# A 16-batch cross-attention and expert feed-forward kernel: the first five steps in another order with products of zeros, and the output projection in front of the scores from step 6

## The chip, the core and the metric

One core of a Trainium2 chip runs the kernel. Its engines each work through a queue of their own: TensorE (PE; PEld is its weight load), VectorE (DVE), ScalarE (ACT), GpSimd (POOL) and SyncE (SP), which here only issues transfers (DMAs). The metric is the time of one execution on the device in microseconds (us), as the median of several runs.

## The reference

For each of 16 batches, with 256 tokens and 128 features:

```python
x = x + xattn(layernorm(x), ctx, ctx, Wq, bq, Wk, bk, Wv, bv, Wo, bo)   # 16 heads of 8 features, 64 keys
h = layernorm(x)
e = argmax(h.mean(axis=1) @ Wr + br)                                    # one expert of 8 for the whole batch
x = x + relu(h @ W1[e] + c1[e]) @ W2[e] + c2[e]                         # 512 hidden features
```

Everything is float32.

## The kernel before, in words

The work is a pipeline by hand. Each engine has a program of its own, written as a loop over steps t = -3 to 21, and in each step it does its share of several batches at different stages; semaphores tie the engines together. In step t, TensorE does for batch t the score product whose maximum is wanted (`scores_for_max`, L627, into banks a to d of PSUM), for batch t-2 the product of probabilities and V (`heads_product`, L645, into bank_g), for batch t-1 the scores that go to the exponential (`scores_t`, L682, banks e, f, a, b), for batch t-3 the output projection (`project_o`, L695, bank_g), for batch t+1 the projection of q (`project_q`, L708), the transposes of maxima and layernorms (L723, L749, L784), and for batch t-5 the two products of the expert (`up` L735, `down` L763). RAMP = 5 separates the first steps, in which the projection of q stands earlier, from the others.

The maximum takes a way of its own: VectorE reduces the scores (`reduce_max`, L877), TensorE transposes the result, ScalarE copies it (`max_transposed`, L514), and SyncE sends it into `q_stack`, whose rows are the operand of `scores_t`. There q stands split in a high and a low part (`high_q` L483 on ScalarE, `low_q` L937 on VectorE), also sent by SyncE. `q_stack` has two buffers. K is split in the same way in four pieces of four batches (`project_k`, `high_k`, `low_k`, `stack_k`), placed per head in `k_all` (`place_k`) and masked into `k_diag` (`diag_k`, on GpSimd and, for the last piece, ScalarE). V is projected in four pieces (`project_v` L603) and copied by ScalarE (`v_of` L460) into a frame that GpSimd fills first (`fill_v` L381).

ScalarE in a step t of 5 and more: the copy of the heads out of bank_g (`copy_heads` L498, batch t-2), the exponentials of batch t-1 in four groups (L490), `high_q`, `max_transposed`, four relus of batch t-5 (L530), a first layernorm (`normalise_x` L474), and copies of transposes. SyncE then takes the heads apart into `denom` and `numer` (`split_heads`); VectorE inverts (`invert_sums` L946), GpSimd multiplies (`normalise_heads` L398). VectorE adds the output projection to x plus bias (`add_x1` L903) and takes statistics; GpSimd makes the second layernorm of them (`norm2`, L359 to L368), and that is transposed (L784), summed for the choice of the expert (`logits`, `route_best`), and multiplied by the weights of the expert, which SyncE has loaded (`load_expert`).

What sets the order around the change is the order of the calls in each engine's loop, and the waits in front of each call. `project_o` has these, and they are not changed:

```python
pe.wait_ge(attn_done, n + 1)
if live(n + 1):
    pe.wait_ge(heads_out, n + 2)
```

`heads_out` counts the copies of the heads by ScalarE: the projection of batch t-3 waits for the copy of batch t-2 in the same step, as the projection writes bank_g, which that copy reads. `transpose_max` waits for the first two exponentials of batch t-1, since it shares bank_f with the scores.

Of the kernel before, what the change touches and what calls it, by code (L numbers as in the profile page):

```python
# [6 lines left out]
F32 = mybir.dt.float32  # L7
F32R = mybir.dt.float32r
# [23 lines left out]
def xattn_moe_kernel(nc, x, ctx_t, consts, experts, out):  # L32
# [13 lines left out]
    with ExitStack() as ctx:  # L46
# [8 lines left out]

        cst = sb("cst", [P, CONST_W])
# [4 lines left out]
        eps_sb = sb("eps_sb", [P, QT])  # L61
        table_in = sb("table_in", [P, QT])
# [13 lines left out]
        q_stack = sb("q_stack", [P, 2, SLOTS, TOK], F32R)  # L76
# [9 lines left out]
        numer = sb("numer", [P, TOK])  # L86
        denom = sb("denom", [P, TOK])
# [39 lines left out]
        def flat(bank):  # L127
# [5 lines left out]
        STATS_AT = {-3: (0, 1), -1: (2,), 0: (3, 4), 1: (5, 6), **{t: (t + 5,) for t in range(2, B - 5)}}  # L133
        SCALE_AT = {-3: ((0, 1), (1, 2)), -1: ((2, 3),), 0: ((3, 4),), 1: ((4, 6),),
                    **{t: ((t + 4, t + 5),) for t in range(2, B - 4)}}
        XN_AT = {0: (2,), 1: (3,), 2: (4,), 3: (5, 6), **{t: (t + 3,) for t in range(4, B - 3)}}
        RAMP = 5

        def late(n):
            return n + 4 < RAMP  # L140

# [5 lines left out]
        kstack_in = [sem(f"kstack_in{k}") for k in range(B // PIECE)]  # L147
        qstack_in = [sem(f"qstack_in{k}") for k in range(2)]
        max_in = [sem(f"max_in{k}") for k in range(2)]
# [6 lines left out]
        qzero_done = sem("qzero_done")  # L156
        klo_done = sem("klo_done")
# [20 lines left out]
        kdiag_act = sem("kdiag_act")  # L178
# [23 lines left out]

        half_set = sem("half_set")
# [15 lines left out]

        def live(n):  # L220
            return 0 <= n < B

# [6 lines left out]
        def _(sp):  # L229
# [9 lines left out]
            def stack_k(c):  # L239
                cols = cols_of(c)  # L240
                if c == 0:
                    sp.wait_ge(kzero_dve, 1)
                else:
                    sp.wait_ge(kzero_pool, 1)
                sp.wait_ge(khi_done, c + 1)
                for row in range(2):
                    sp.dma_start(k_stack[row::4, :, cols], k_parts[:, 0, cols].bitcast(F32)
                                 ).then_inc(kstack_in[c], 16)
                sp.wait_ge(klo_done, c + 1)
                sp.dma_start(k_stack[2::4, :, cols], k_parts[:, 1, cols].bitcast(F32)).then_inc(kstack_in[c], 16)  # L250

            def stack_q_high(n):
                par = n % 2
# [3 lines left out]
                if n >= 2:  # L257
                    sp.wait_ge(s_done, GROUPS * (n - 1))
                for row in (0, 2):
                    sp.dma_start(q_stack[row::4, par].bitcast(F32), q_parts[:, par, 0, :].bitcast(F32)  # L260
# [787 lines left out]
```

## Time and profile before

| what | value |
|---|---|
| median of 3 runs | 180.39 us (179.39 to 180.77) |
| the profiled execution's own time | 179.66 us |
| its span, first to last instruction | 177.8 us |
| TensorE busy | 147.7 us, 83% of the span |
| VectorE, ScalarE, GpSimd busy | 121.5, 113.9, 105.2 us |
| mean granted TensorE clock | 0.914 of full |

The span is from the first instruction to the last; the execution's own time has 1.9 us more around it. Busy time is an average over three stages: the first steps, the steady steps and the end. A granted clock of 1.00 is 2.4 GHz, of 0.50 is 1.2 GHz. In a row of the timeline the square brackets say how long the engine had been idle before, and what ended that.

### The profile page before, as it was taken

To read this page: it belongs to the slowest core of one execution; us is meant where nothing else is said; L and a number is where in the kernel's file an instruction comes from. 1 tells how busy PE (TensorE), PEld (TensorE's weight loads), DVE (VectorE), ACT (ScalarE), POOL (GpSimd) and SP (SyncE) were. 2 spreads that over 40 slices of the span, in tenths; PEclk is the share of its full clock that TensorE was granted. 3 is DMA by queue.
4 is the path that set the end of the run, shared out by engine and by line. 5 is a ranking of instruction groups with operands and counts; after the bars stand their busy time and mean duration, and the time that the engine had idled before them with its cause. 6 is when DMAs were issued, how large, how long until landed. Compare 5 with 4: busy or idle time off the path is not lost.

```text
span 177.8 us, 4066 instructions
## 1 busy us (share of the span) xinstructions
PE 147.7 (83%) x1194; PEld 108.8 (61%) x1194; DVE 121.5 (68%) x334; ACT 113.9 (64%) x281; POOL 105.2 (59%) x186
## 2 busy tenths in 40 slices
PE   0495678748873999999999999999999989878893
PEld 0273344416342687777778787787877667566583
DVE  6694846283926889898979989797786937263200
ACT  3325565858876597896969778696766748234340
POOL 6567279311908485959586685956648293676300
PEclk9998755795765699999999999999999999999999
DMA  5838324492024254647455553646556452454150
GB/s 171 204 137 250 119 94 151 96 316 70 30 94 139 90 182 163 195 128 238 142 192 187 175 196 133 217 123 236 166 183 197 149 166 81 161 176 128 66 168 30
DMA packets 25014, 27.27 MB, mean 153 GB/s; under 512 B 4512, under 2 KB 20768, under 8 KB 24992
## 3 DMA queue, kind: packets, MB, share of 16 engines
q1 hardware_dynamic: 23136, 26.13, 45.3%
q10 hardware_dynamic: 1856, 0.88, 1.9%
q8 instruction: 10, 0.16, 0.4%
q14 instruction: 12, 0.10, 0.2%
HBM read 12.58 MB, written 2.10 MB: 83 GB/s over the span
## 4 chain that ended last, share of the span: by engine, by line
PE 65%; ACT 11%; DVE 5%; POOL 5%; issue 5%; DMA 5%; SPq 2%; ACTq 0%; POOLq 0%; DVEq 0%
PE bank_g L763 15%; PE bank_g L645 9%; PE bank_c L735 6%; PE bank_q L708 5%; PE bank_g L695 5%; PE bank_a L627 4%; PE bank_e L682 4%; PE bank_d L735 4%; ACT probs_t L490 3%; POOL xn L368 3%; DMA x_sb<-in_x 3%; PE bank_a L682 2%; ACT hid_t L530 2%; DMA ew<-in_experts 2%; PE bank_e L749 2%
## 5 line engine op out<-in xcount | busy, mean ns | idle before, releaser
L763 PE MATMUL bank_g<-ew,hid_t 128*128 128x128 f32 x256 | 32.4, 280 | 2.1 <-ACT hid_t L530 2.0
L763 PEld LDWEIGHTS bank_g<-ew,hid_t 128*128 128x128 f32 x256 | 29.8, 192 | 6.6 <-issue 6.0
L946 DVE RECIPROCAL inv_sum<-denom 128x256 f32<-128x256 f32 x16 | 27.7, 1731 | 0.2
L368 POOL TENSOR_SCALAR xn<-x,mv,rstd 128x128 f32<-128x128 f32 x32 | 25.2, 795 | 1.7
L359 POOL TENSOR_TENSOR ve<-mv,eps_sb 128x2 f32<-128x2 f32 x16 | 3.1, 195 | 38.3 <-DVE mv L916 38.3
L645 PE MATMUL bank_g<-probs_t,v_all 128*32 128x256 f32 x256 | 19.6, 430 | 1.6 <-DVE k_parts L840 1.2
L867 DVE TENSOR_TENSOR y_sb<-bank_g,x_b 128x256 f32<-128x256 f32 x16 | 6.8, 425 | 20.1 <-PE bank_g L763 20.1
L498 ACT COPY heads_sb<-bank_g 128x512 f32<-128x512 f32 x16 | 9.4, 586 | 16.5 <-PE bank_g L645 16.4
L530 ACT ACTIVATE hid_t<-bank_c,ew 128x256 f32<-128x256 f32 x32 | 13.4, 472 | 8.6 <-PE bank_c L735 8.3
L405 POOL TENSOR_TENSOR x_b<-x,ew 128x256 f32<-128x256 f32 x16 | 11.6, 727 | 10.9 <-DMA ew<-in_experts 10.4
L735 PE MATMUL bank_c<-xn_t,ew 128*128 128x256 f32 x64 | 16.7, 383 | 0.0
L735 PE MATMUL bank_d<-xn_t,ew 128*128 128x256 f32 x64 | 16.4, 379 | 0.0
L506 ACT ACTIVATE xn_t<-bank_f 128x256 f32<-128x256 f32 x16 | 6.1, 382 | 16.0 <-PE bank_f L784 16.0
L877 DVE TENSOR_REDUCE negmax<-bank_a 128x8 f32<-128x512 f32 x16 | 10.9, 682 | 6.6 <-PE bank_d L627 6.6
L398 POOL TENSOR_TENSOR attn_t<-numer,inv_sum 128x256 f32<-128x256 f32 x16 | 11.7, 730 | 4.2 <-DVE inv_sum L946 4.2
L530 ACT ACTIVATE hid_t<-bank_d,ew 128x256 f32<-128x256 f32 x32 | 13.4, 470 | 0.0
L695 PE MATMUL bank_g<-cst,attn_t 128*128 128x128 f32 x64 | 12.4, 320 | 1.1 <-ACT heads_sb L498 0.8
L735 PEld LDWEIGHTS bank_d<-xn_t,ew 128*128 128x128 f32 x64 | 12.2, 191 | 1.6
L708 PE MATMUL bank_q<-xn_t,cst 128*128 128x256 f32 x32 | 12.3, 471 | 0.5 <-ACT xn_t L520 0.5
L903 DVE TENSOR_TENSOR x<-bank_g,x_bo 128x256 f32<-128x256 f32 x16 | 6.5, 405 | 8.8 <-PE bank_g L695 7.6
L474 ACT ACTIVATE xn<-x_sb,shift,rstd 128x128 f32<-128x128 f32 x28 | 12.1, 486 | 0.0
L362 POOL TENSOR_TENSOR rstd<-ve,minus_half 128x2 f32<-128x2 f32 x16 | 11.3, 709 | 1.3
(81 smaller groups left out, 402.6 us busy)
## 6 DMA issues: line engine op xcount, KB each, us to landing
q_stack<-q_parts SPq DMA_DIRECT2D x48, 128.0 KB, 2.2
ew<-in_experts SPq DMA_DIRECT2D x16, 320.0 KB, 3.1
ew<-in_experts SPq DMA_DIRECT2D x16, 258.0 KB, 2.7
denom<-heads_sb SPq DMA_DIRECT2D x16, 128.0 KB, 2.1
numer<-heads_sb SPq DMA_DIRECT2D x16, 128.0 KB, 2.1
out_y<-y_sb SPq DMA_DIRECT2D x16, 128.0 KB, 2.0
k_stack<-k_parts SPq DMA_DIRECT2D x12, 128.0 KB, 2.4
x_sb<-in_x SPq DMA_DIRECT2D x2, 768.0 KB, 5.4
```

The costliest lines, as they stand in the source:

```text
L362: nc.gpsimd.tensor_tensor(rstd2[:, par], ve2[:, par], minus_half[:].unsqueeze(2), ALU.pow).then_inc(rstd2_done, 1)
L368: nc.gpsimd.tensor_scalar(xn2[:, par, q, :], x1[:, par, q, :], mv2[:, par, q, 0:1], rstd2[:, par, q, :], ALU.subtract, ALU.mult).then_inc( ...
L398: nc.gpsimd.tensor_tensor(attn_t[:], numer[:], inv_sum[:], ALU.mult).then_inc(attn_done, 1)
L405: nc.gpsimd.tensor_tensor(x1_b2[:], x1[:, par], b2_of(par).unsqueeze(1).to_broadcast([P, QT, D]), ALU.add).then_inc(x1b2_done, 1)
L474: nc.scalar.activation(xn1[:, n, q, :], x_sb[:, n, q, :], ACT.Identity, bias=shift1[:, n, q, :], scale=rstd1[:, n, q, :]).then_inc(xn1_act, 1)
L530: nc.scalar.activation(hid_t[:, c, :], UP_BANK[half][:, c % 2, :], ACT.Relu, bias=b1_of(par, c)).then_inc(hid_done, 1)
L645: mm = nc.tensor.matmul(bank_g[32 * tile:32 * (tile + 1), a, :], v_all[:, n, c].rearrange("p r k -> p (r k)"), probs_t[:, c, :], start=Tru ...
L695: mm = nc.tensor.matmul(bank_g[:, 0, q * P:(q + 1) * P], attn_t[:, q * P:(q + 1) * P], const("wo_t"), start=True, stop=True)
L708: nc.tensor.matmul(bank_q[:, 1, :], const("wq_t"), xn1_t[:], start=True, stop=True).then_inc(q_proj, 1)
L735: mm = nc.tensor.matmul(UP_BANK[half][:, c % 2, :], ew[:, par, c * P:(c + 1) * P], xn2_t[:, par, :], start=True, stop=True)
L763: mm = nc.tensor.matmul(bank_g[:, 0, q * P:(q + 1) * P], hid_t[:, c, q * P:(q + 1) * P], w2_of(par, c), start=(c == 0 and q == 0), stop=(c ...
L946: nc.vector.reciprocal(inv_sum[:], denom[:]).then_inc(inv_done, 1)
```

## The change

TensorE gets products of a tile of zeros (`keep_busy`): four at the start and two behind the first K projection, two at the end of steps 0 to 4, one in front of the scores in steps 1 to 5. The first layernorm's transpose moves from the step before to right in front of the projection of q, the transpose of the maxima behind the scores (in bank_d for the first five batches), K is projected in three pieces (4, 4 and 8 batches) in steps -2 and 0, V in steps 0, 1 and 2. `q_stack` gets a third buffer, `numer` and `denom` a second one. On ScalarE the exponentials of the first steps stand in two halves around the copy of the maxima; the last two K diagonals go to GpSimd. On VectorE the reciprocal of batches 0 and 1 moves one step later, between two halves of the maximum. On GpSimd the second layernorm stands last in the step, behind the scale of the first layernorm and the sum of x and bias. From step 6 on, `project_o` stands in front of `scores_t`. The second layernorm of batch 1 is transposed at the front of step 5.

```diff
 # TensorE
+            def keep_busy(bank, times):
+                for _ in range(times):
+                    nc.tensor.matmul(bank[:, 1, :], zeros[:, 0:P], zeros[:], start=True, stop=True)
+
+            pe.wait_ge(zeros_set, 1)
+            keep_busy(bank_f, 4)
...
             for t in STEPS:
                 if t == -2:
                     project_k(0)
+                    keep_busy(bank_f, 2)
                 if live(t):
                     scores_for_max(t)
+                if live(t - 4) and not late(t - 4) and not ending(t - 4):
+                    transpose2(t - 4)
                 if live(t - 2):
                     heads_product(t - 2)
                 if live(t + 1) and t < RAMP:
+                    transpose1(t + 1)
                     project_q(t + 1)
...
-                if live(t) and t < RAMP:
-                    transpose_max(t)
-                if live(t - 4) and not late(t - 4):
-                    logits(t - 4)
-                if live(t - 1):
-                    scores_t(t - 1)
-                if live(t - 3):
+                if live(t - 4) and not late(t - 4):
+                    logits(t - 4)
+                if live(t - 3) and t > RAMP:
+                    project_o(t - 3)
+                if 1 <= t <= RAMP:
+                    keep_busy(bank_e, 1)
+                if live(t - 1):
+                    scores_t(t - 1)
+                if live(t) and t < RAMP:
+                    transpose_max(t)
+                if t == 0:
+                    project_k(2)
+                if t == 1:
+                    project_v(1)
+                if live(t - 3) and t <= RAMP:
                     project_o(t - 3)
                 if t == 2:
-                    project_k(3)
-                if t in (2, 3):
-                    project_v(t)
+                    project_v(2)
+                    project_v(3)
+                if 0 <= t < RAMP:
+                    keep_busy(bank_c, 2)
...
 # ScalarE, its loop
                 if live(t + 1) and t < RAMP:
+                    xn1_transposed(t + 1)
                     high_q(t + 1)
...
+                if live(t - 1):
+                    exp_group(t - 1, 0)
+                    exp_group(t - 1, 1)
                 if live(t) and t < RAMP:
                     max_transposed(t)
-                if t < RAMP:
-                    for n in XN_AT.get(t, ()):
-                        normalise_x(n)
                 if live(t - 1):
-                    for g in range(GROUPS):
-                        exp_group(t - 1, g)
+                    exp_group(t - 1, 2)
+                    exp_group(t - 1, 3)
...
 # VectorE, its loop
                 if t == -2:
                     normalise_x(0)
                     dve.wait_ge(cst_in[0], 16)
                     place_k()
+                if t == -1:
+                    low_k(0)
                     normalise_x(1)
-                    low_k(0)
...
+                if live(t - 3) and t < RAMP:
+                    invert_sums(t - 3)
...
 # GpSimd, its loop
-                if live(t - 3):
-                    norm2(t - 3)
                 for a, b in SCALE_AT.get(t, ()):
                     scale1(a, b)
                 if live(t - 2):
                     add_bo(t - 2)
+                if live(t - 3):
+                    norm2(t - 3)
                 if t == -3:
                     pool.wait_ge(cst_in[0], 16)
                     fill_v(0)
+                    zero_q()
...
-        STATS_AT = {-3: (0, 1), -1: (2,), 0: (3, 4), 1: (5, 6), **{t: (t + 5,) for t in range(2, B - 5)}}
+        STATS_AT = {-3: (0,), -2: (1,), 0: (2, 3), 1: (4, 5), 2: (6, 7), **{t: (t + 5,) for t in range(3, B - 5)}}
```

TensorE's queue in a steady step (step 6), before; rows that come twice stand once, L645 is the heads product, L659 the logits, L682 the scores, L695 the output projection:

```order
L645 MATMUL bank_g<-probs_t,v_all 32x256 x8
L659 MATMUL bank_q<-cst,tok_sum 1x8
L682 MATMUL bank_e<-q_stack,k_diag 128x256
L682 MATMUL bank_f<-q_stack,k_diag 128x256
L682 MATMUL bank_a<-q_stack,k_diag 128x256
L682 MATMUL bank_b<-q_stack,k_diag 128x256
L695 MATMUL bank_g<-cst,attn_t 128x128 x2
L708 MATMUL bank_q<-xn_t,cst 128x256
L723 MATMUL bank_f<-cst,negmax 16x128 x2
```

The same place in the changed kernel (L687 heads product, L701 logits, L737 output projection, L724 scores, L750 projection of q):

```order
L687 MATMUL bank_g<-probs_t,v_all 32x256 x8
L701 MATMUL bank_q<-cst,tok_sum 1x8
L737 MATMUL bank_g<-cst,attn_t 128x128 x2
L724 MATMUL bank_e<-q_stack,k_diag 128x256
L724 MATMUL bank_f<-q_stack,k_diag 128x256
L724 MATMUL bank_a<-q_stack,k_diag 128x256
L724 MATMUL bank_b<-q_stack,k_diag 128x256
L750 MATMUL bank_q<-xn_t,cst 128x256
L759 MATMUL bank_f<-cst,negmax 16x128 x2
```

The output projection (bank_g from attn_t) moved from behind the eight products of the scores to in front of them; all else stands as before.

TensorE's queue in step 1, from the projection of q on, before (L593 and L603 project K and V, L723 transposes the maxima, L749 the first layernorm):

```order
L708 MATMUL bank_q<-xn_t,cst 128x256
L593 MATMUL bank_g<-ctx_sb,cst 128x256
L603 MATMUL bank_g<-cst,ctx_sb 64x64 x8
L723 MATMUL bank_f<-cst,negmax 16x128 x2
L682 MATMUL bank_e<-q_stack,k_diag 128x256
L682 MATMUL bank_f<-q_stack,k_diag 128x256
L682 MATMUL bank_a<-q_stack,k_diag 128x256
L682 MATMUL bank_b<-q_stack,k_diag 128x256
L749 MATMUL bank_e<-cst,xn 128x128 x2
```

And in the changed kernel (L785 transposes the first layernorm, L617 are the products of zeros, L724 the scores, L759 the transpose of the maxima, L642 a projection of V):

```order
L785 MATMUL bank_e<-cst,xn 128x128 x2
L750 MATMUL bank_q<-xn_t,cst 128x256
L617 MATMUL bank_e<-zeros 128x256
L724 MATMUL bank_e<-q_stack,k_diag 128x256
L724 MATMUL bank_f<-q_stack,k_diag 128x256
L724 MATMUL bank_a<-q_stack,k_diag 128x256
L724 MATMUL bank_b<-q_stack,k_diag 128x256
L759 MATMUL bank_d<-cst,negmax 16x128 x2
L642 MATMUL bank_g<-cst,ctx_sb 64x64 x8
L617 MATMUL bank_c<-zeros 128x256 x2
```

The transpose of the layernorm now stands in front of the projection of q, the transpose of the maxima behind the scores, the K projection is gone from here, and zeros stand in front of the scores and at the end.

VectorE's queue at the start, before (L925 and L929 are the statistics for the first layernorm, L858 the layernorm, L847 the placing of K):

```order
L925 BN_STATS stats<-x_sb 128x6 x2
L929 BN_AGGR mv<-stats 128x2 x2
L925 BN_STATS stats<-x_sb 128x6 x2
L929 BN_AGGR mv<-stats 128x2 x2
L858 TENSOR_SCALAR xn<-x_sb,mv,rstd 128x128 x2
L847 TENSOR_SCALAR k_all<-k_parts,cst 128x256 x3
L858 TENSOR_SCALAR xn<-x_sb,mv,rstd 128x128 x2
```

And in the changed kernel (L968, L972, L901 and L890 in the same parts):

```order
L968 BN_STATS stats<-x_sb 128x6 x2
L972 BN_AGGR mv<-stats 128x2 x2
L901 TENSOR_SCALAR xn<-x_sb,mv,rstd 128x128 x2
L890 TENSOR_SCALAR k_all<-k_parts,cst 128x256 x3
L968 BN_STATS stats<-x_sb 128x6 x2
L972 BN_AGGR mv<-stats 128x2 x2
L883 SCALAR_TENSOR_TENSOR k_parts<-bank_g,cst,k_parts 128x256
L901 TENSOR_SCALAR xn<-x_sb,mv,rstd 128x128 x2
```

The layernorm of batch 0 moved in front of the statistics of batch 1.

## Rows read from the trace of the kernel before

**Rows 1.** The page, 2: TensorE's granted clock in 40 slices of the span.
```profile
PEclk9998755795765699999999999999999999999999
```

**Rows 2.** Windows: stretch, length, busy us (instructions) of PE, PEld, DVE, ACT, POOL, clock, DMA.
```profile
10.70:66.18 55.48, 40.58 (x306) 25.72 (x306) 35.22 (x95) 37.64 (x88) 30.70 (x54) 0.72 0.43 137
66.18:137.10 70.92, 70.09 (x630) 54.89 (x629) 61.09 (x165) 55.10 (x142) 49.36 (x91) 1.00 0.54 179
137.10:177.80 40.70, 33.16 (x253) 25.93 (x252) 17.42 (x54) 17.82 (x46) 19.18 (x30) 1.00 0.40 127
97.98:105.82 7.84, 7.82 (x74) 6.14 (x74) 7.04 (x21) 6.22 (x16) 5.76 (x12) 1.00 0.53 178
```

**Rows 3.** Windows of one us each, same columns.
```profile
38.00:39.00 1.00, 0.00 (x0) 0.00 (x0) 1.00 (x2) 0.00 (x0) 0.00 (x0) 1.00 1.08 375
41.00:42.00 1.00, 1.00 (x7) 0.78 (x6) 0.00 (x0) 1.00 (x4) 0.00 (x0) 0.50 0.00 0
...
46.00:47.00 1.00, 1.00 (x16) 0.30 (x8) 1.00 (x3) 1.00 (x3) 0.92 (x3) 0.50 0.00 0
47.00:48.00 1.00, 1.00 (x8) 0.58 (x4) 1.00 (x3) 0.70 (x3) 0.92 (x4) 1.00 0.00 0
```

**Rows 4.** Timeline of a steady step: start us, us, engine, line, operation.
```profile
98.34 1.07 PE L645 MATMUL bank_g<-probs_t,v_all 128*32 128x256 f32 x16
99.36 0.38 PE L682 MATMUL bank_e<-q_stack,k_diag 64*128 64x256 f32 x1
99.48 0.58 ACT L498 COPY heads_sb<-bank_g 128x512 f32<-128x512 f32 x1 [0.99 <-PE bank_g L645]
99.96 0.60 ACT L490 ACTIVATE probs_t<-bank_e 128x512 f32<-128x512 f32 x1
100.25 0.71 PE L695 MATMUL bank_g<-cst,attn_t 128*128 128x128 f32 x4
100.80 0.60 PE L708 MATMUL bank_q<-xn_t,cst 128*128 128x256 f32 x2
102.60 0.84 ACT L530 ACTIVATE hid_t<-bank_c,ew 128x256 f32<-128x256 f32 x2
103.58 2.02 PE L763 MATMUL bank_g<-ew,hid_t 128*128 128x128 f32 x16
```

**Rows 5.** Timeline near the end, step 17.
```profile
153.51 0.58 ACT L498 COPY heads_sb<-bank_g 128x512 f32<-128x512 f32 x1 [0.67 <-PE bank_g L645]
154.24 0.68 PE L695 MATMUL bank_g<-cst,attn_t 128*128 128x128 f32 x4 [0.78 <-ACT heads_sb L498]
```

**Rows 6.** Timeline, scores of step 1 and q projection of step 2.
```profile
22.19 0.35 PE L682 MATMUL bank_e<-q_stack,k_diag 64*128 64x256 f32 x1 [0.81 <-ACT negmax_t L514]
22.70 0.60 ACT L490 ACTIVATE probs_t<-bank_e 128x512 f32<-128x512 f32 x1
...
27.51 1.22 PE L708 MATMUL bank_q<-xn_t,cst 128*128 128x256 f32 x2
```

**Rows 7.** Timeline of the start, VectorE and GpSimd.
```profile
6.91 0.57 DVE L858 TENSOR_SCALAR xn<-x_sb,mv,rstd 128x128 f32<-128x128 f32 x2
8.01 1.16 POOL L381 COPY v_all<-cst 128x1024 f32<-128x1024 f32 x1
8.19 1.33 DVE L858 TENSOR_SCALAR xn<-x_sb,mv,rstd 128x128 f32<-128x128 f32 x2
```

**Rows 8.** The page, 5 and 6, and two timeline rows of ScalarE.
```profile
L368 POOL TENSOR_SCALAR xn<-x,mv,rstd 128x128 f32<-128x128 f32 x32 | 25.2, 795 | 1.7
L359 POOL TENSOR_TENSOR ve<-mv,eps_sb 128x2 f32<-128x2 f32 x16 | 3.1, 195 | 38.3 <-DVE mv L916 38.3
...
q_stack<-q_parts SPq DMA_DIRECT2D x48, 128.0 KB, 2.2
...
33.28 0.81 ACT L460 COPY v_all<-bank_g 64x256 f32<-64x256 f32 x2 [0.61 <-PE bank_g L603]
...
39.84 1.64 ACT L474 ACTIVATE xn<-x_sb,shift,rstd 128x128 f32<-128x128 f32 x4
```

More of the change, by code:

```diff
@@ L218, in xattn_moe_kernel, with maxt_bank, k_bank, k_cols @@
         STEPS = range(-3, B + 6)
+        def maxt_bank(n):
+            return bank_d if n < RAMP else bank_f
         def live(n):
             return 0 <= n < B
+        KGROUPS = [(0, PIECE), (PIECE, 2 * PIECE), (2 * PIECE, B)]
+        def k_bank(g):
+            return flat(bank_f) if g == 2 else bank_g[:, 1, :]
+        def k_cols(g):
+            return slice(KGROUPS[g][0] * KEYS, KGROUPS[g][1] * KEYS)
+        def v_bank(c):
+            return bank_g[:, c // 3, :]
         def cols_of(c):
@@ L317, in _ @@
                     stack_q_low(t + 1)
+                if live(t - 4) and late(t - 4):
+                    load_expert(t - 4)
                 if t == -2:
@@ L564, in _ @@
                     relu(t - 5, 1)
-                if t >= RAMP:
-                    for n in XN_AT.get(t, ()):
-                        normalise_x(n)
-                if live(t + 2):
+                for n in XN_AT.get(t, ()):
+                    normalise_x(n)
+                if live(t + 2) and t >= RAMP - 1:
                     xn1_transposed(t + 2)
                 if t in (2, 3):
-                    place_k(t - 1, range(SLOTS))
-                if t == 4:
-                    diag_k(0)
-                    diag_k(1)
-                if t in (5, 6):
-                    place_k(3, (2 * t - 10, 2 * t - 9))
-                if live(t - 3) and not late(t - 3):
+                    place_k(2, (2 * t - 4, 2 * t - 3))
+                if t in (4, 5):
+                    place_k(3, (2 * t - 8, 2 * t - 7))
+                if live(t - 3) and ending(t - 3):
                     xn2_transposed(t - 3)
@@ L652, in logits @@
                 pe.wait_ge(xn2t_done, n + 1)
-                if late(n):
+                if late(n) and n + 4 < RAMP:
                     pe.wait_ge(qlo_done, n + 6)
@@ L668, in scores_t @@
                 else:
[L669 to L671 removed]
+                    pe.wait_ge(kdiag_done, 8)
+                if n == 0:
+                    pe.wait_ge(klo_done, 3)
                 pe.wait_ge(xn1t_done, min(n + 3, B))
                 for shalf in range(2):
[L674 removed]
+                    if shalf == 0 and n >= 3:
                         pe.wait_ge(xn2t_done, n - 2)
@@ L683, in scores_t @@
                                                   k_diag[rows, slot, n].rearrange("p h k -> p (h k)"),
-                                                  q_stack[rows, par, slot, :], start=True, stop=True)
+                                                  q_stack[rows, buf, slot, :], start=True, stop=True)
                             if low == 1:
@@ L789, in _ @@
                     project_k(0)
+                    keep_busy(bank_f, 2)
                 if live(t):
                     scores_for_max(t)
+                if live(t - 4) and not late(t - 4) and not ending(t - 4):
+                    transpose2(t - 4)
                 if live(t - 2):
@@ L828, in _ @@
                     down(t - 5, 1)
-                if live(t - 3) and not late(t - 3):
+                if live(t - 3) and ending(t - 3):
                     transpose2(t - 3)
```

235 lines of the change are left out of this document (119 added, 116 removed).

## The prediction

> **What bounds the kernel now.** I read the granted clock first, then the windows by stage, then one steady step in the timeline, then the end. The row of clock digits [rows 1] is below 9 in ten of the first 14 slices and stays at full afterwards. The windows [rows 2] are cut where TensorE starts the score product for the maximum (L627) of step 0 (10.70), step 6 (66.18) and step 15 (137.10). The first six steps take 55.5 us at a mean clock of 0.72 with TensorE busy 40.6 us; the nine steps behind them take 70.9 us with TensorE busy 70.1; the end takes 40.7. One steady step is 7.84 us with TensorE busy 7.82. So the early part waits, and runs much of its work at the half level of 1.2 GHz; the middle is TensorE without a gap. The clock's rows [rows 3] show the pattern: after a stretch with nothing on TensorE (38 to 39) it is at half from 41 on, and after work without a pause (46 to 47) it is back at full.
>
> In the steady step a second engine is as tight as TensorE [rows 4]. Counted from the start of the heads product (L645, 98.34): scores (L682) +1.02, ScalarE's copy of the heads (L498) +1.14, first exponential (L490) +1.62, output projection (L695) +1.91, first relu (L530) +4.26, down product (L763) +5.24. From the first exponential to the first relu ScalarE works without a gap (four exponentials, the split of q, the maxima: 2.64), and the down product starts 0.98 behind the first relu. The output projection now stands behind the scores, and these 0.89 us cover ScalarE's copy of the heads, on which the projection waits because both use bank_g. In the last steps, where no scores stand between, that wait is seen bare [rows 5]: copy at 153.51, projection at 154.24, that is 0.73 later, with TensorE idle 0.78.
>
> **Second part of the change: output projection in front of the scores, from step 6.** Nothing is added; the order turns round. Again from the heads product: copy +1.14 as before; the projection 0.73 behind it, +1.87; it occupies TensorE 0.55 (100.25 to 100.80 [rows 4]), so the scores start at +2.42, not +1.02. With the clock at full the first exponential starts 0.51 behind the scores (22.19 to 22.70 [rows 6]): +2.93, not +1.62. ScalarE's 2.64 and the 0.98 follow unchanged: down product +6.55, not +5.24. TensorE does nothing else from there to the next step. A step grows by 1.31, to 9.15. What the earlier projection could give back is the second layernorm; but its sum (L903) stands in VectorE's queue behind the maxima, whose start has not moved, and GpSimd waits 38.3 us in all for VectorE's statistics already [rows 8], so nothing comes earlier that anyone waits for. Nine steps from step 6 to step 15: 9 x 9.15 = 82.4 against 70.9, **+11.4**. Bounds of the term: none of ScalarE's chain delayed, +0.65 a step (rival 2); the wait of 0.78 and the projection's 0.55 both in full, +1.33. I take 1.31, as the chain is shown gapless.
>
> Steps 15 and 16 have the same order: no projection of q in step 15, the maxima are late anyway, I work out +1.2 and +1.3. At the very end the addition of the bias to x now stands in front of the layernorm on GpSimd, not behind it, so the last two projections come earlier; I count 0.8 (between nothing and the 1.16 of GpSimd's larger copy [rows 7]). That makes **+1.7** for the end (1.3 to 2.5).
>
> **First part: steps 0 to 5.** 21 products of zeros come in: six before the first step, two at the end of steps 0 to 4, one in front of the scores in steps 1 to 5. One occupies TensorE like the projection of q, which has the same shape: 0.60 at full (0.43 to the next start), 1.22 at half [rows 4, 6]. The pairs at a step's end lie beside the exponentials, on which the next step waits: nothing, at full clock. The single ones stand in front of scores whose operands have landed (the copies to q_stack take 2.2 us [rows 8] and are issued over 3 us earlier): 0.43 each on the path, 2 us in all, and 5 if at half. Their gain is the clock.
>
> I laid the steps out with these durations, engine by engine, at full clock. The start: the first layernorm (L858) need no longer wait for the statistics of batch 1, but lands beside GpSimd's fill of V, which now comes right behind the scale of batch 0. The trace has this pairing once: two layernorm instructions took 0.57 alone and 1.33 beside that copy [rows 7]; **+0.8**, on the path to the first maximum. The maxima (four reductions), the K projection, now 512 columns in step 0, and two zeros then put step 1 at 16.5.
> The Trainium skill, SBUF — State Buffer, "Who interferes with whom", says that GpSimd and VectorE share a pair of ports as a lock, and that the second to issue stands still until the first is through. The copy's 1.16 beside the 1.33 fits it; by the rule the new fill of the third q_stack buffer right behind would hold VectorE's placing of K too, an estimate of up to 0.9 more, and the total would be 188.6.
>
> A step of this part is then one chain: product for the maximum 0.43, heads product to copy 1.14, copy 0.48, transposed x and q projection about 1.0, zeros 0.43, scores to exponential 0.51, four exponentials with the maxima between 2.4, and 0.3 of handing on: 6.7. Step 1 waits for the layernorm of batch 2 behind the K placing on ScalarE: 7.2. Step 2: 6.7. In steps 3 and 4 ScalarE first has V copies, layernorms and K placing left from the step before (0.81 for two, 1.64 for four [rows 8]): 7.9 and 7.7. In step 5 TensorE stands before the transpose of batch 1's second layernorm (two of 795 ns on GpSimd [rows 8], and its statistics ahead of them): a wait of 2.1, 10.6 in all. 16.5 + 7.2 + 6.7 + 7.9 + 7.7 + 10.6 = 56.6 for the start of step 6, against 66.18.
>
> But the pauses are not gone: before the transpose in step 1 (2 us), in step 3 (1 us twice), in step 5 (2 us) of the layout. Before, the clock fell after such pauses [rows 3], and no zeros stand in these: the zeros are in the queue behind the instruction that waits. For each I count one burst at half: projection of q +0.6 (1.22 less 0.60 [rows 4, 6]), one zero +0.6, first half of the scores +0.3, that is 1.5; three of them 4.5. Bounds: none (clock held), or 2.5 each. Step 6 starts at 61.1, a **gain of 5.1**; between 9.6 and 2.
>
> Edits with one answer, nothing: third q_stack buffer and second numerator and denominator (waits of SyncE's queue, off this path); K in three pieces (three copies fewer to issue); the last K diagonals on GpSimd, not ScalarE (four of them stand in front of the first product of heads with the reciprocal; my layout ends them 0.3 before it, and 1.6 of slack follow); loading of the first expert behind the copies of q (needed a step later). If the GpSimd cover is gone, up to 1 us in step 3.
>
> **Sum.** Against the profiled execution's own 179.66 (span 177.8, 1.9 around it): -5.1 + 11.4 + 1.7 = +8.0, 187.7. That execution lies 0.4% below the median of 180.39, so there is 0.7 of scatter on top; I say **187.5**.
>
> **Rivals.**
> 1. The clock holds through the first steps, since fewer and shorter pauses are left than before. For: zeros fill the stretches between the pauses, which were broken up before. Against: [rows 3], and the zeros stand behind the waits. Then 187.7 - 4.5 = 183.2, still 1.5% slower.
> 2. The move costs only TensorE's pause, as ScalarE has slack (place: first relu to down product, steps 6 to 15). Then a step pays 0.85 for the copy less some 0.2 that the scores no longer wait for a maximum: 0.65, or 5.5 for nine steps, and 0.3 at the end: 180.4 with the pauses of the clock, 175.9 with the clock held: faster. It decides from 0.7 us of slack in that place. For: ScalarE is not busy all the step, it waits before the copy of the heads. Against: that pause lies outside the chain, and from the first exponential on I see none.
> 3. The zeros do not do what they say: products of zeros occupy TensorE and do not raise the clock. Then step 6 starts at 66.2 plus five zeros at 1.02: +5.1 + 11.4 + 1.7, 198. Against: the clock rose after any work without pause; no row shows zeros.
>
> **How the numbers follow.** Forecast 0.59 (184 to 191.5 by the bounds of the bursts and the end). Rival 1 0.17 (181 to 184.5; a quarter of it within 1%). Rival 2 0.19 (0.11 faster, 0.08 within 1%). Rival 3 0.05. About 1% is what a measurement of this kernel can tell from no change. Faster 0.11, within 1% 0.04 + 0.08 = 0.12, slower 0.59 + 0.13 + 0.05 = 0.77. The range runs from 181 to 191.5: the forecast, rival 1 and the upper edge of rival 2; it leaves out rival 3 and most of rival 2.
>
> **What would show it.** Right: in a steady step TensorE idle 0.7 to 0.85 in front of the output projection, released by the copy of the heads; the first exponential some 2.9 behind the heads product; a period near 9.1; the down product released by the relu; step 6 starting between 57 and 64; low clock digits still in the first third. Wrong: a period of 8.5 or less (rival 2), step 6 before 56, or the clock at half through the first steps in spite of the zeros (rival 3).

## The result and the profile after

The changed kernel takes 189.38 us (median of 4 runs, 188.22 to 190.11) against 179.89 (4 runs, 178.58 to 180.77) for the kernel before: 1.053 of it, 95% interval 1.043 to 1.062. It is slower by 5.3%; 187.5 had been forecast, with a range of 181 to 191.5. The profiled execution took 190.11 us, the longest of the four, with a span of 188.3.

First the page of the changed kernel: the clock digits, and two of the costliest groups (busy us, mean ns, idle us before them, and what ended it).

```profile
PEclk9975879999969999999999999999999999999999
...
L391 POOL TENSOR_TENSOR ve<-mv,eps_sb 128x2 f32<-128x2 f32 x16 | 3.1, 197 | 28.7 <-DVE mv L959 28.7
...
L737 PE MATMUL bank_g<-cst,attn_t 128*128 128x128 f32 x64 | 10.8, 292 | 9.4 <-ACT heads_sb L526 9.4
```

Five digits of the first 14 are below 9, where ten were [rows 1]: the early clock is better. The second row answers to the idle time of 38.3 us of GpSimd's layernorm [rows 8]; it is now 28.7. The third is new: TensorE stands idle 9.4 us in front of the output projection, released by ScalarE's copy of the heads. In the kernel before it was 1.1:

```profile
L695 PE MATMUL bank_g<-cst,attn_t 128*128 128x128 f32 x64 | 12.4, 320 | 1.1 <-ACT heads_sb L498 0.8
```

The windows of the changed kernel, cut at the start of the score product (L668) of steps 0, 6 and 15, with the columns of [rows 2]:

```profile
10.10:62.39 52.29, 41.66 (x335) 26.77 (x335) 37.09 (x100) 35.26 (x87) 34.31 (x57) 0.87 0.45 151
62.39:145.22 82.83, 71.77 (x630) 54.75 (x629) 61.45 (x165) 55.10 (x140) 49.35 (x88) 1.00 0.46 154
145.22:188.30 43.08, 32.83 (x253) 25.89 (x252) 17.54 (x54) 18.04 (x46) 18.47 (x28) 1.00 0.35 113
```

Step 6 starts 3.8 us earlier (62.39, before 66.18), the nine steady steps take 11.9 more (82.83, before 70.92), the end 2.4 more (43.08, before 40.70). That is +10.5, the whole difference of the two spans (188.3 and 177.8). In the middle the number of TensorE's instructions is the same 630. Its busy time has risen by 1.7 us (71.77, before 70.09); the other 10.2 are gaps.

One steady step of the changed kernel in the timeline (step 7, heads product at 72.03), to be laid beside [rows 4]:

```profile
72.03 1.07 PE L687 MATMUL bank_g<-probs_t,v_all 128*32 128x256 f32 x16
...
73.17 0.59 ACT L526 COPY heads_sb<-bank_g 128x512 f32<-128x512 f32 x1 [0.99 <-PE bank_g L687]
73.90 0.68 PE L737 MATMUL bank_g<-cst,attn_t 128*128 128x128 f32 x4 [0.78 <-ACT heads_sb L526]
74.51 0.38 PE L724 MATMUL bank_e<-q_stack,k_diag 64*128 64x256 f32 x1
...
75.05 0.60 ACT L518 ACTIVATE probs_t<-bank_e 128x512 f32<-128x512 f32 x1 [1.30 <-PE bank_e L724]
75.18 0.70 PE L750 MATMUL bank_q<-xn_t,cst 128*128 128x256 f32 x2
75.55 0.59 ACT L518 ACTIVATE probs_t<-bank_f 128x512 f32<-128x512 f32 x1
...
76.28 0.38 PE L759 MATMUL bank_f<-cst,negmax 128*16 128x128 f32 x2 [0.40 <-ACT probs_t L518]
76.50 1.03 PE L771 MATMUL bank_c<-xn_t,ew 128*128 128x256 f32 x4
...
77.64 0.84 ACT L558 ACTIVATE hid_t<-bank_c,ew 128x256 f32<-128x256 f32 x2
...
78.63 2.02 PE L799 MATMUL bank_g<-ew,hid_t 128*128 128x128 f32 x16
```

From the heads product: copy +1.14, output projection +1.87, scores +2.48, first exponential +3.02, down product +6.60. In the kernel before, the down product stood at +5.24; the step has grown by the same 1.36, from 7.84 to 9.20. There are two gaps on TensorE, 0.78 in front of the output projection and 0.40 in front of the transpose of the maxima (L759), which shares bank_f with the second exponential. The waits over all nine steady steps (us in total, times, longest):

```profile
PE bank_g L737 <- ACT heads_sb L526: 7.0, 9, 0.8
...
PE bank_f L759 <- ACT probs_t L518: 3.6, 9, 0.4
...
PE bank_g L799 <- ACT hid_t L558: 0.2, 1, 0.2
```

7.0 + 3.6 = 10.6 of the 11.9 us. The down product, in the last row, hardly waits for the relus.

Last the start, VectorE and GpSimd, against [rows 7]:

```profile
5.80 1.04 POOL L413 COPY v_all<-cst 128x1024 f32<-128x1024 f32 x1
5.88 2.00 DVE L901 TENSOR_SCALAR xn<-x_sb,mv,rstd 128x128 f32<-128x128 f32 x2 [1.19 <-POOL rstd L378]
6.79 0.95 POOL L366 MEMSET q_stack<- 128x1024 f32 x1
7.80 0.86 DVE L890 TENSOR_SCALAR k_all<-k_parts,cst 128x256 fp32r<-128x256 f32 x3
```

The first layernorm takes 2.00 us, not 0.57, and the next VectorE instruction starts as GpSimd's second fill ends (6.79 + 0.95 = 7.74).

### The profile page after: what moved, and what is told of

It reads as the page before. It is cut to its first block, busy times and chain, and to the rows that moved or that the text cites. A ratio compares the mean times of both kernels' runs of the same rounds, so it can differ in the third digit from the quotient of the medians.

```text
span 188.3 us, 4135 instructions
## 1 busy us (share of the span) xinstructions
PE 152.9 (81%) x1234; PEld 111.9 (59%) x1234; DVE 123.1 (65%) x333; ACT 111.7 (59%) x278; POOL 108.8 (58%) x186
## 4 chain that ended last, share of the span: by engine, by line
PE 58%; ACT 22%; issue 8%; DVE 6%; POOL 5%; ACTq 0%; POOLq 0%
PE bank_g L799 15%; ACT probs_t L518 9%; PE bank_g L687 8%; PE bank_c L771 6%; PE bank_g L737 5%; ACT heads_sb L526 4%; PE bank_d L771 4%; PE bank_e L724 4%; PE bank_q L750 3%; POOL xn L400 3%; PE bank_a L668 2%; ACT hid_t L558 2%; PE bank_f L759 2%; PE bank_f L815 2%; ACT xn L502 2%
## 5 line engine op out<-in xcount | busy, mean ns | idle before, releaser
L518 ACT ACTIVATE probs_t<-bank_e 128x512 f32<-128x512 f32 x16 | 9.6, 597 | 17.8 <-PE bank_f L724 13.9
L391 POOL TENSOR_TENSOR ve<-mv,eps_sb 128x2 f32<-128x2 f32 x16 | 3.1, 197 | 28.7 <-DVE mv L959 28.7
L687 PE MATMUL bank_g<-probs_t,v_all 128*32 128x256 f32 x256 | 18.0, 400 | 1.5 <-issue 0.8
L737 PE MATMUL bank_g<-cst,attn_t 128*128 128x128 f32 x64 | 10.8, 292 | 9.4 <-ACT heads_sb L526 9.4
L980 DVE SCALAR_TENSOR_TENSOR q_parts<-bank_q,cst,q_parts 128x256 fp32r<-128x256 f32 x16 | 7.7, 482 | 14.9 <-ACT q_parts L511 14.9
L750 PE MATMUL bank_q<-xn_t,cst 128*128 128x256 f32 x32 | 12.1, 463 | 4.2 <-ACT xn_t L548 4.2
L737 PEld LDWEIGHTS bank_g<-cst,attn_t 128*128 128x128 f32 x64 | 8.3, 190 | 10.6 <-issue 10.4
```

The costliest lines, as they stand in the source:

```text
L518: nc.scalar.activation(probs_t[:, 2 * g:2 * g + 2, :], SCORE_BANK[g][:], ACT.Exp, scale=SCALE).then_inc(exp_done, 1)
L687: mm = nc.tensor.matmul(bank_g[32 * tile:32 * (tile + 1), a, :], v_all[:, n, c].rearrange("p r k -> p (r k)"), probs_t[:, c, :], start=Tru ...
L737: mm = nc.tensor.matmul(bank_g[:, 0, q * P:(q + 1) * P], attn_t[:, q * P:(q + 1) * P], const("wo_t"), start=True, stop=True)
L750: nc.tensor.matmul(bank_q[:, 1, :], const("wq_t"), xn1_t[:], start=True, stop=True).then_inc(q_proj, 1)
```

## The experiments

Runs are called by their first letter where that is plain (run a is a_scores_first). The kernel before was timed again beside each group of runs, with medians of 178.79 to 179.71 us; each ratio is to the times of its own group, and the square brackets behind it are its 95% interval.

**Scores first everywhere (a_scores_first).** The move of the output projection undone, the first part kept:

```diff
-                if live(t - 3) and t > RAMP:
-                    project_o(t - 3)
...
-                if live(t - 3) and t <= RAMP:
+                if live(t - 3):
                     project_o(t - 3)
```

> The changed kernel with the output projection behind the scores in every step, as before the change. Theory: the projection in front exposes ScalarE's copy of the heads and moves scores, exponentials and the expert's products back by 1.3 us in each of the nine steady steps, and about 1 us more in the end. Then the steady period goes from 9.2 back to 7.84 and the time from 189.4 to between 175.5 and 178 us, faster than the kernel before by 1 to 2.5%. Rival: the longer period comes from something else in the change (the third q_stack buffer, GpSimd's second layernorm standing last, the split numerator): the period stays above 8.5 and the time above 183.

Measured: 174.08 us (173.22 to 175.24, 4 runs), 0.975 of the kernel before [0.966, 0.983]. The windows by stage, and the clock:

```profile
PEclk9996999999996999999999999999999999999999
```

```profile
10.11:60.04 49.93, 38.88 (x335) 25.36 (x335) 37.01 (x100) 35.31 (x87) 34.38 (x57) 0.93 0.48 158
60.04:131.21 71.17, 70.17 (x630) 54.83 (x630) 61.20 (x165) 54.53 (x140) 48.95 (x88) 1.00 0.53 174
131.21:171.40 40.19, 32.95 (x253) 25.89 (x252) 17.52 (x54) 17.84 (x46) 18.63 (x29) 1.00 0.39 129
```

The middle is back at 71.2 us and the time a little below the expected 175.5 to 178. The rival, a longer period from another edit, falls. The first part alone is a gain of 2.5% (1.7 to 3.4 by the interval); moving the output projection turns it into a loss.

**Output projection first alone (b_output_first).** The kernel before with that one move:

```diff
+                if live(t - 3) and t > RAMP:
+                    project_o(t - 3)
                 if live(t - 1):
                     scores_t(t - 1)
-                if live(t - 3):
+                if live(t - 3) and t <= RAMP:
                     project_o(t - 3)
```

> The kernel before with one edit: from step 6 on the output projection stands in front of the scores. Theory: the period goes from 7.84 to 9.2 and the time from 179.9 to 192 to 194.5 us, 12 to 14 us more. Rival (only TensorE's pause of 0.65 a step counts, and ScalarE's exponentials have slack): period 8.5, time 185 to 187.

Measured: 194.58 us (194.19 to 195.28, 4 runs), 1.087 [1.078, 1.095]. Middle and end:

```profile
66.83:150.04 83.21, 71.88 (x629) 54.77 (x628) 61.33 (x165) 55.78 (x142) 50.39 (x92) 1.00 0.47 156
150.04:193.20 43.16, 33.02 (x253) 25.90 (x252) 17.54 (x54) 18.01 (x46) 18.42 (x28) 1.00 0.35 113
```

+12.3 in the middle and +2.5 in the end, as in the changed kernel. The two parts act on different stages and nearly add up: the move costs 15.8 us by this run (194.58 less 178.79) and 15.3 by run a (189.38 less 174.08).

**Work in the pause (d_q_in_pause).** The changed kernel, with the projection of q moved into the gap:

```diff
+                if live(t + 1) and t > RAMP:
+                    project_q(t + 1)
                 if live(t - 3) and t > RAMP:
                     project_o(t - 3)
...
-                if live(t + 1) and t >= RAMP:
+                if live(t + 1) and t == RAMP:
                     project_q(t + 1)
```

> The changed kernel with the projection of q, from step 6 on, in front of the output projection, where TensorE waits 0.78 us for the copy of the heads. Theory: the start of the scores, not TensorE's pause, sets the step by way of ScalarE's exponentials; the pause is filled by 0.43 us of work, but scores still start 2.4 us behind the heads product, so the period stays within 0.1 of 9.2 and the time within 1 us of 189.4. Rival: TensorE's pause is the cost; period 8.75, time 185 to 186 us.

Measured: 190.16 us, 1.059 [1.050, 1.069], the same as the changed kernel within the intervals. A steady step of it:

```profile
88.91 1.07 PE L687 MATMUL bank_g<-probs_t,v_all 128*32 128x256 f32 x16
...
90.53 0.67 PE L750 MATMUL bank_q<-xn_t,cst 128*128 128x256 f32 x2 [0.53 <-DVE route L930]
91.03 0.61 PE L737 MATMUL bank_g<-cst,attn_t 128*128 128x128 f32 x4
91.57 0.38 PE L724 MATMUL bank_e<-q_stack,k_diag 64*128 64x256 f32 x1
...
93.34 0.38 PE L759 MATMUL bank_f<-cst,negmax 128*16 128x128 f32 x2 [1.03 <-ACT probs_t L518]
```

The profiled execution took 193.56 us, the second longest of five; its nine middle steps ran at full clock, and its end was longer, 47.0 us where the changed kernel has 43.1. The gap in front of the output projection is gone; the gap in front of the maxima has grown from 0.40 to 1.03. The projection of q waits for VectorE's read of the logits in the same bank, so the scores start 2.66 behind the heads product, 0.18 later than in the changed kernel, and the period is 9.38, 0.18 longer (expected: within 0.1 of 9.2). So period and start of the scores move together, as they do from the kernel before to the changed kernel. Rival 2 of the prediction, in which TensorE's pause alone is the cost, is refuted: it has a period of 8.5, and here one of 8.75. The test is not a clean one, since the projection of q brings a wait of its own, 0.53 us, into the place that it was to fill.

**Maxima behind the up product (j_max_behind_up).** This takes TensorE's second wait away:

```diff
 # TensorE (on ScalarE max_transposed moves behind the relus in the same way)
-                if live(t) and t >= RAMP:
+                if live(t) and t == RAMP:
                     transpose_max(t)
                 if live(t - 5):
                     up(t - 5, 0)
                     up(t - 5, 1)
+                if live(t) and t > RAMP:
+                    transpose_max(t)
```

> The changed kernel with the transpose of the maxima (and ScalarE's copy of it) behind the expert's up product (behind the relus), from step 6 on. Theory: in the changed kernel TensorE waits a second time, 0.40 us in front of the transpose of the maxima, for the second exponential, and is busy from there to the end of the step, so that this wait and not the relus carries the delay on: period from 9.2 to 8.7 to 8.85, total 184.5 to 186.5. Rival (the chain of the prediction: four exponentials, split of q, maxima, relu, down product, with the relus as the bound): only the copy of the maxima leaves the chain, 0.2 to 0.35 at most; period 8.85 to 9.05, total 186 to 188.5.

Measured: 188.64 us (187.39 to 190.14, 4 runs), 1.055 [1.044, 1.065]. One row of the step and TensorE's waits over the nine steady steps:

```profile
103.11 2.02 PE L801 MATMUL bank_g<-ew,hid_t 128*128 128x128 f32 x16 [0.30 <-ACT hid_t L558]
```

```profile
PE bank_g L739 <- ACT heads_sb L526: 7.0, 9, 0.8
...
PE bank_g L801 <- ACT hid_t L558: 2.9, 9, 0.5
```

The period falls to 8.92 (60.67 to 140.97 in nine steps), by the rival's amount; the total lies 0.1 above the rival's range. The wait of 0.40 is gone and one of 0.3 for the relus stands in its place. Two chains end nearly together here: in the changed kernel the second exponential releases TensorE last, and ScalarE's chain to the relus is right behind. A cost of 1.08 us a step against the kernel before stays even so (8.92 less 7.84). The 2.5 us won in the middle are mostly given back in the end (44.8 us from step 15 on, 43.1 before), where the late maxima were not looked into.

**No zeros (c_no_zeros).** Run a_scores_first with `range(0)` for `range(times)` in `keep_busy`.

> The kernel with scores first (run a_scores_first) without any product of zeros. Theory: the zeros raise the clock in the first six steps; without them step 6 starts 2 to 5 us later, and the total is 178.5 to 182 us. Rival: the granted clock falls after the same pauses with or without them, and each zero on the path only costs: step 6 starts 0 to 2 us earlier, and the total is 175 to 177.5.

Measured: 176.80 us (174.10 to 180.18, 5 runs), 0.988 [0.978, 0.997]. The profiled execution was its fastest:

```profile
PEclk9999969999855999999999999999999999999999
```

```profile
10.96:61.23 50.27, 36.70 (x304) 23.32 (x304) 36.49 (x100) 35.36 (x87) 33.83 (x56) 0.86 0.47 157
```

The total lies in the rival's range, but step 6 starts 1.2 later than in run a (61.23 against 60.04), not earlier. TensorE does 2.2 us less work in the first six steps, and they still take 0.3 longer.

The clock in the row and the window is too high at the start of this run. The projections of q of batches 0 and 1:

```profile
9.18 1.22 PE L750 MATMUL bank_q<-xn_t,cst 128*128 128x256 f32 x2 [0.46 <-ACT xn_t L548]
...
13.03 1.22 PE L750 MATMUL bank_q<-xn_t,cst 128*128 128x256 f32 x2 [0.46 <-ACT xn_t L548]
```

In run a the same products take 0.70 (at 8.84 and 12.69), so without zeros TensorE runs at half here, where the digits say 9. The products for the maximum are still slow at 18.32 (0.58, later 0.38). With half clock up to there, 7.7 us, the mean clock of the first six steps is not the 0.86 of the window but about 0.78, an estimate from these durations; with zeros it is 0.93. In the kernel before the window's 0.72 [rows 2] is a little too high in the same way: its projection of q at 11.43 takes 1.22.

So the zeros do raise the clock: its mean over a whole execution is 0.961 to 0.980 in the four of run a and 0.895 to 0.960 in the five of run c. What that is worth is not settled: 0.9 us between the fastest executions of runs a and c (173.22 and 174.10), 2.7 between their medians, and the two intervals overlap. The new order brings a gain without them: in the fastest execution the first six steps fall from 55.5 to 50.3, and the median is 2.0 us below the kernel before, where run a has 4.7.

**GpSimd's fills later (e_fill_later).** `fill_v(0)` and `zero_q()` at `t == -2`, not -3, in run a_scores_first.

> Run a_scores_first with GpSimd's fill of V and of the third q_stack buffer one step later, behind the scale of batch 1. Theory: the first layernorm on VectorE takes 2.01 us there because it lands beside these two fills (0.57 alone); without them it takes under 0.7, step 0 starts at 8.6 to 9.0 instead of 10.11, and the total falls by 0.5 to 1.5 us below that run in the same call or its 174.1. Rival: the layernorm is slow for another reason (its operands, the transfers then running): it stays at 2 us and step 0 at 10.1.

Measured: 174.27 us (172.54 to 176.43, 6 runs), 0.964 [0.956, 0.972]. Its start:

```profile
5.94 0.60 DVE L899 TENSOR_SCALAR xn<-x_sb,mv,rstd 128x128 f32<-128x128 f32 x2 [1.19 <-POOL rstd L378]
...
8.87 0.38 PE L668 MATMUL bank_a<-k_all,q_parts 32*128 32x256 f32 x1 [0.34 <-ACT q_parts L511]
...
9.34 1.93 DVE L899 TENSOR_SCALAR xn<-x_sb,mv,rstd 128x128 f32<-128x128 f32 x1 [0.72 <-POOL rstd L378]
...
11.38 0.69 PE L785 MATMUL bank_e<-cst,xn 128*128 128x128 f32 x2 [2.00 <-DVE xn L899]
```

The theory holds for the layernorm: 0.60 instead of 2.00, and step 0 at 8.87. In the profiled execution the gain does not reach step 6, which starts at 61.74 (run a 60.04): the fills now meet the layernorm of batch 1, one instruction of which takes 1.93, TensorE waits 2.00 for it, and most of step 0 ran at half clock. Whether the total gains is not settled: the medians are the same as in run a (174.27 and 174.08), the ratios are 0.964 and 0.975, and their intervals overlap.

**Both layernorms free (l_fills_last).** The fills behind the first two K diagonals, with the edit of run i_norm_behind below.

> Run i_norm_behind with GpSimd's fills of V (pieces 0 and 1) and of the third q_stack buffer behind the first two K diagonals, where neither of VectorE's first two layernorms runs (in e_fill_later the fills only moved from the first layernorm to the second, which then took over 1.9 us in its place, and the clock fell behind TensorE's wait of 2.0). Theory: both layernorms take about 0.6 us, step 0 starts at 8.9 and step 1 at 16 to 17 with the clock at full, total 170 to 172 us. Rival: step 1 is set by K's placing and the first maxima, the clock falls all the same, and the total is that of i_norm_behind and k_combined, 173.2, within 0.7.

Measured: 173.50 us (170.98 to 175.14, 6 runs), 0.962 [0.956, 0.969]. Both layernorms take 0.60, step 0 starts at 9.00 and step 1 at 16.30, as the theory had it; but in the profiled execution, the longest of the six, the clock fell in steps 0 and 1 (means of 0.77 and 0.61), TensorE waited 2.50 us for the layernorm of batch 2 (1.84 in run a), and step 1 took 10.9 us. The total is the rival's. In this execution the clock, and that wait, took back what the start had won; the shortest of the six took 170.98.

**The layernorm of batch 1 in step 5 (f_norm_late, i_norm_behind, k_combined, g_both).** In run a_scores_first TensorE waits 2.12 us in step 5 for GpSimd, in front of the heads product. f_norm_late sets `LATE = 2`, which puts the transpose and, with it, the choice of the expert and the loading of its weights behind; i_norm_behind moves the transpose and ScalarE's copy of it alone. g_both and k_combined add the later fills of e_fill_later to the one and the other. All four leave out the zero in front of the scores of step 5. On TensorE, i_norm_behind is:

```diff
-                if live(t - 4) and not late(t - 4) and not ending(t - 4):
-                    transpose2(t - 4)
                 if live(t - 2):
                     heads_product(t - 2)
+                if live(t - 4) and not late(t - 4) and not ending(t - 4):
+                    transpose2(t - 4)
```

> Run a_scores_first with the transpose of batch 1's second layernorm behind the heads product of step 5, not in front of it, and without the one zero in front of the scores of step 5. Theory: TensorE's wait of 2.1 us for GpSimd in front of that step is the largest piece left of the first steps, and the fall of the clock in step 5 follows from it; step 5 goes from 12.4 to between 9.5 and 11 us, the clock stays at full there, total 171 to 172.8. Rival: the wait only moves to the scores of batch 4, which need the same transpose: step 5 stays above 11.8 and the total at 173.5 to 175.

> Run a_scores_first with only the transpose of batch 1's second layernorm (and ScalarE's copy of it) behind the heads product of step 5; the choice of the expert stays in front of the scores, other than in f_norm_late; without the one zero of step 5. Theory: in f_norm_late the projection of q waited 2.6 us for the late choice of the expert, which ate the gain; with that gone, step 5 goes from 12.4 to 10 to 11 us and the total to 171 to 173. Rival: TensorE's wait in front of the step was not on the path that sets it (GpSimd's layernorm is needed by the scores of the same step all the same): step 5 stays above 11.8, total 173.5 to 175.

> Both edits, of e_fill_later and f_norm_late. Theory: they add up, at different places: total 170 to 172 us, 4 to 5% below the kernel before. Rival: the earlier start is waited away by step 1, on the placing of K; total as f_norm_late alone.

> Run i_norm_behind with the later fills of e_fill_later as well: the kernel that should beat both. Theory: step 0 at 8.9 and step 5 near 10.5, total 170.5 to 172.5, 4 to 5% below the kernel before. Rival: the earlier start is lost to a fall of the clock in step 0, as in e_fill_later, and the total is that of i_norm_behind within 0.5 us.

Measured: f_norm_late 179.01 us, 0.992 [0.987, 0.996]; g_both 179.23, 0.998 [0.993, 1.004]; i_norm_behind 173.24, 0.963 [0.955, 0.972]; k_combined 173.25, 0.964 [0.956, 0.972]. f_norm_late failed because the choice of the expert went behind it: in step 5 the projection of q waits for VectorE's read of the logits.

```profile
57.25 1.19 PE L750 MATMUL bank_q<-xn_t,cst 128*128 128x256 f32 x2 [2.64 <-DVE route L926]
```

Step 5 takes 14.75 us there, and step 6 still 9.68. With the choice of the expert in place, step 5 of k_combined takes 11.66 us (48.11 to 59.77), not 12.45 and not the expected 10.5. Two other waits stand in it, GpSimd's for the weights of the first expert (1.78 in run a) and TensorE's for the layernorm of batch 2:

```profile
53.94 0.73 POOL L437 TENSOR_TENSOR x_b<-x,ew 128x256 f32<-128x256 f32 x1 [2.40 <-DMA ew<-in_experts]
...
59.40 0.44 PE L815 MATMUL bank_f<-cst,xn 128*128 128x128 f32 x2 [1.38 <-POOL xn L400]
```

Step 0 of k_combined starts at 11.06, not at the expected 8.9: in this execution the projection of q in front of it ran at half (1.22 us at 9.28).

**GpSimd's old order from step 6 on (h_norm_first).** In run a_scores_first, `norm2` in front of `scale1` and `add_bo` for t > RAMP.

> Run a_scores_first with GpSimd's second layernorm, from step 6 on, in front of the scale of the first one and the sum of x and bias, as before the change. Theory: in the steady steps it has slack, period 7.84 as it is; in the last steps the sum of x and bias stands on the way to the last output projections, and the end (step 15 to the last instruction) goes from 40.2 to 40.7 to 41 us. Rival: the order on GpSimd sets nothing anywhere; end within 0.2 of 40.2.

Measured: 175.99 us (174.08 to 176.96, 4 runs), 0.976 [0.966, 0.985], period 7.84. From the output projection of step 17 to that of step 18 it takes 6.13 us (150.39 to 156.52), 5.88 in run a_scores_first and 6.52 before the change; in h_norm_first and before, that projection waits 0.2 us for GpSimd, in a_scores_first not at all. The order is worth 0.3 to 0.6 us there. The end as a whole was 42.3, which neither text has. TensorE waits in it 0.77 and 1.13 us for a second layernorm, and not in run a; but GpSimd waits for experts' weights in both ends, so the rest isn't laid to the order.

The fastest versions are i_norm_behind, k_combined, l_fills_last and e_fill_later, 3.6 to 3.8% below the kernel before. Among themselves, and from a_scores_first, the intervals don't part them.

## Why the prediction was right

**Steady steps, +11.4 forecast, +11.9 measured.** The steps of the sum hold one by one: copy +1.14 (forecast +1.14), projection +1.87 (+1.87), scores +2.48 (+2.42), first exponential +3.02 (+2.93), down product +6.60 (+6.55), period 9.20 (9.15). The projection occupies 0.61 where 0.55 was taken. Runs a and b show that the move makes this by itself. One link was named wrong: the down product was to be released by the relu. It is TensorE's own queue, started by the second exponential at the transpose of the maxima; run j shows the relus coming right behind, so the sum came out alike. In run d the step grew by as much as the scores were late, 0.18, so no slack lies between the scores and the step's end, which was the point against rival 2.

**End, +1.7 forecast, +2.4 measured.** The heads-to-down stretches of steps 15 and 16 grew by 1.39 each (1.2 and 1.3 forecast), by the down products' starts in the changed kernel and in run a. The credit of 0.8 for GpSimd's order was mis-sized: the whole end of run a is 0.5 shorter than before, and run h puts the order at 0.3 to 0.6.

**First steps, a gain of 5.1 forecast, 3.8 measured, and 6.1 in run a with the same code up to there.** The forecast for step 6, 61.1, lies between these two executions (62.39, the longest of the changed kernel's four, and 60.04, the shortest of run a's four). Its parts, from the starts of the score products in the timelines:

| step | forecast, full clock | changed kernel | a_scores_first | before |
|---|---|---|---|---|
| start of step 1 | 16.5 | 19.33 | 17.96 | 16.92 |
| 1 | 7.2 | 8.25 | 7.27 | 7.99 |
| 2 | 6.7 | 6.84 | 6.83 | 8.69 |
| 3 | 7.9 | 7.91 | 7.90 | 11.15 |
| 4 | 7.7 | 7.63 | 7.63 | 12.19 |
| 5 | 10.6 | 12.43 | 12.45 | 9.24 |

Steps 1 to 4 came as laid out wherever the clock was full. Two terms failed and nearly cancelled, so that the gain came out near the forecast is luck. Of the three bursts at half, only the one in step 5 is there in both executions (12.4 against 10.6, 1.8 where 1.5 was taken); the one in step 1 is there in the changed kernel alone (8.25 against 7.2), and step 3 has none. And step 0 was too short: the pairing of the layernorm with GpSimd was priced at 0.8 and cost 1.4 (2.00 less 0.57), and a fall of the clock in step 0 was not counted. The rule cited in the prediction from the Trainium skill (SBUF — State Buffer, "Who interferes with whom") came out nearer: the second fill did hold VectorE, though it was the layernorm and not the placing of K that it held. That its total of 188.6 lies nearer to 189.38 as well is partly luck, since bursts that did not come and the longer end go into it too.

Rival 1, the clock held throughout, is not what the page shows, though run a comes near it. Rival 3 is not borne out: the mean clock of every execution with zeros (run a) is above that of every one without (run c). But the rival's price was too high: it gives the new order no gain without a higher clock, and run c starts step 6 at 61.23, the kernel before at 66.18. How much of the gain is the zeros' stays open.

## What to carry to other kernels

An instruction that is to be moved forward may now stand bare in front of a wait that other work used to cover; price the wait, then follow the engine it delays to the step's end, and look whether that chain has slack. Filling the bare gap with other work gained nothing here (run d), as the instruction behind it still set the step. Do not take a better clock for a shorter time: the zeros raised the clock, and what they won is not clear of the scatter (run c). Judge the parts of a change apart: here 2.5% won in the first steps and 8.7% lost behind them (run b) came in one change.

## What the runs showed of the hardware

Two GpSimd fills back to back held one VectorE layernorm for both of their lengths (1.04 and 0.95): 2.00 us, 0.60 without them (runs e and l). The first of the layernorm's two instructions alone takes 1.94, from 5.88 to 7.82. The rule of the Trainium skill (SBUF — State Buffer, "Who interferes with whom"), an exclusive lock, fits; that a chain of two keeps it is what the trace adds.

The same code doesn't always get the same clock. In steps 0 and 1 the changed kernel and run a are one program, and TensorE waits 1.18 us for the second layernorm in both; afterwards, windows of the changed kernel:

```profile
12.00:13.00 1.00, 0.54 (x3) 0.14 (x2) 1.00 (x4) 0.37 (x1) 1.00 (x1) 0.50 0.39 135
...
17.00:18.00 1.00, 1.00 (x2) 0.34 (x1) 0.57 (x2) 0.64 (x2) 0.00 (x0) 0.50 0.60 207
```

and of run a:

```profile
12.00:13.00 1.00, 0.54 (x3) 0.30 (x2) 1.00 (x4) 0.37 (x1) 1.00 (x1) 1.00 0.39 135
...
17.00:18.00 1.00, 1.00 (x9) 0.61 (x7) 0.97 (x7) 0.80 (x2) 0.17 (x1) 1.00 0.79 274
```

The one is at half from 12 to 18, the other only from 13 to 16. Step 1 starts 1.4 us apart in the two, more than most edits of the first steps were worth.

The two executions differ before that. The first K projection and the first layernorm's transpose, in the changed kernel:

```profile
5.41 0.67 PE L629 MATMUL bank_g<-ctx_sb,cst 128*128 128x256 f32 x2 [0.54 <-DMA ctx_sb<-in_ctx_t]
...
7.93 0.44 PE L785 MATMUL bank_e<-cst,xn 128*128 128x128 f32 x2 [0.99 <-DVE xn L901]
```

and in run a:

```profile
5.13 1.19 PE L629 MATMUL bank_g<-ctx_sb,cst 128*128 128x256 f32 x2 [0.26 <-DMA ctx_sb<-in_ctx_t]
...
7.94 0.44 PE L785 MATMUL bank_e<-cst,xn 128*128 128x128 f32 x2 [0.59 <-DVE xn L899]
```

In the changed kernel the K projection already ran at full (0.67), in run a still at half (1.19), and the pause behind it was longer (0.99, in run a 0.59). So the rise to full came earlier in the changed kernel, and so did the fall. Why the rise comes at different times, no run here shows.
